# Matmuls without a reader in the last chunk's drain, and other places for the key differences

## The reference, cut to what matters

```python
x = x + attn_a(layernorm(x))   # 16 heads of 16; keys and values at offsets 0..40, 96, 128, 384 back
x = x + ffn(layernorm(x))      # 8 groups of 512 tokens: (x W1^T + b1) W2^T + b2
x = x + attn_b(layernorm(x))   # per head softmax(rope(q) rope(k)^T / 4) v over all 2048 keys
x = x + ffn(layernorm(x))
```

## Time and profile before

| | |
|---|---|
| median of 3 runs | 2109.53 us (2108.59 to 2109.8) |
| the profiled execution | 2115.02 us, span from first to last instruction 2112.9 us |
| mean granted clock | 0.965 |
| TensorE busy | 1989.9 us (94%) |
| VectorE busy | 1792.2 us (85%) |
| ScalarE busy | 1570.7 us (74%) |
| GpSimd busy | 777.9 us (37%) |
| first instruction of the second stage on TensorE | at 846.5 us |

### The profile page before, as it was taken

One profiled execution on the slowest core, in us unless ns is written; L12 is line 12 of the kernel. 1 busy time (PEld: TensorE's weight loads), 2 busy tenths in 40 slices (PEclk: granted clock), 3 DMA queues, 4 the chain that ended last, 5 costly groups with the idle time before them and its releaser, 6 DMA issues. The chain is left out here.

```text
span 2112.9 us, 48657 instructions
## 1 busy us (share of the span) xinstructions
PE 1989.9 (94%) x18498; PEld 770.3 (36%) x18498; DVE 1792.2 (85%) x3187; ACT 1570.7 (74%) x3827; POOL 777.9 (37%) x1040
## 2 busy tenths in 40 slices
PE   7889999899998786999999999999999999999978
PEld 5444555454554332222222222222222222322333
DVE  3797888788897676899999999999999999999356
ACT  0155676566664321999999999999999999999911
POOL 2599899799998310720203003003000000052100
PEclk9999999999999866899999999999999999999989
DMA  8465566566655541511102002001010010041311
GB/s 280 131 135 125 127 153 134 137 152 132 154 137 119 141 96 51 112 33 27 36 5 55 8 7 56 7 14 49 5 27 4 6 26 5 7 126 47 111 63 60
DMA packets 230728, 163.81 MB, mean 78 GB/s; under 512 B 153256, under 2 KB 201432, under 8 KB 230488
## 3 DMA queue, kind: packets, MB, share of 16 engines
q1 hardware_dynamic: 198416, 112.70, 22.2%
q0 software_dynamic: 15616, 32.02, 5.9%
q10 hardware_dynamic: 16464, 15.98, 2.3%
HBM read 98.43 MB, written 45.16 MB: 68 GB/s over the span
## 5 line engine op out<-in xcount | busy, mean ns | idle before, releaser
L1498 ACT ACTIVATE pr<-ps_s 128x512 f32<-128x512 f32 x2048 | 1042.8, 676 | 1.7 <-PE ps_s L1396 1.6
L1515 DVE TENSOR_REDUCE mx<-ps_m 128x1 f32<-128x512 f32 x1472 | 932.1, 684 | 45.3 <-PE ps_m L1373 41.5
L1414 PE MATMUL ps_o<-pr,vg 128*32 128x256 f32 x8192 | 655.0, 392 | 9.3 <-ACT f_ou L1478 8.6
L1396 PE MATMUL ps_s<-qs,ks 50*128 50x512 f16 x2048 | 612.4, 384 | 9.4 <-PEq L322 9.3
L1373 PE MATMUL ps_m<-ks,qs 48*128 48x512 f16 x1716 | 544.6, 384 | 0.0
L597 POOL TENSOR_TENSOR room<-qs 128x512 f32<-128x512 f32 x336 | 416.4, 1272 | 92.0 <-ACT qs L864 53.6
L1325 POOL DMA_DIRECT2D vg<-vb_d x24 | 19.7, 821 | 943.4 <-PE ps_o L1414 862.9
L1414 PEld LDWEIGHTS ps_o<-pr,vg 128*32 128x32 f32 x8192 | 162.5, 108 | 333.8 <-issue 210.0
L1373 PEld LDWEIGHTS ps_m<-ks,qs 48*128 48x128 f16 x1716 | 142.3, 93 | 353.3 <-issue 203.7
L943 DVE TENSOR_TENSOR room<-PSa,qs 128x512 f32<-128x512 f32 x368 | 234.4, 678 | 15.4 <-PE PSa L690 15.0
L690 PE MATMUL PSa<-room,sj 128*32 128x512 f32 x1408 | 199.1, 613 | 11.7 <-issue 4.7
(11 more groups left out here) (175 smaller groups left out, 2201.5 us busy)
## 6 DMA issues: line engine op xcount, KB each, us to landing
room<-skew SPq DMA_DIRECT2D x128, 208.0 KB, 4.0
skew<-attn SPq DMA_DIRECT2D x64, 164.0 KB, 5.0
tail_room<-in_W SPq DMA_DIRECT2D x32, 256.0 KB, 3.5
tail_room<-in_W2T SPq DMA_DIRECT2D x32, 256.0 KB, 4.1
vb_d<-vb SPq DMA_DIRECT2D x8, 1024.0 KB, 5.9
qs<-ks SPq DMA_DIRECT2D x26, 256.0 KB, 5.4
ks<-k_d POOLq DMA_DIRECT2D x48, 128.0 KB, 3.2
qs<-q_d POOLq DMA_DIRECT2D x180, 32.0 KB, 2.8
```

The source lines that it names most:

```text
L1396: pe.matmul(ps_s[:, op % SB, :], ks[rows, slot, j // 2, kt * P:(kt + 1) * P], qs[rows, q, j // 2, :], start=True, stop=True).then_inc(s_ps, 1)
L1414: mm = pe.matmul(ps_o[SLOT * j:SLOT * (j + 1), cols], vg[:, kt, j, :], pr[:, kt % PR_RING, j, cols], start=(kt == 0 and part == 0), stop=( ...
L1498: act.activation(pr[:, kt % PR_RING, j, :], ps_s[:, place_of(y, n) % SB, :], ACT.Exp, scale=exp_scale).then_inc(p_ready, 1)
L1515: dve.tensor_reduce(best, ps_m[:, n % M_BANKS, :], AX_X, ALU.max).then_inc(m_read, 1)
```

## The change

Two things. First, on ScalarE the steps `diff` go from positions 68.9 and 69 to 75.7 and 75.8, `diff_last` from 76.8 and 77.2 to 78.8 and 78.9; on VectorE `diff` goes from 71.9 and 72 to 79.5 and 80.5, `diff_rest` from 74.8 and 75 to 82 and 82.1. In whole positions ScalarE's `diff` of chunk 1 moves from 92.9 to 99.7, past `scores` 0 and 1 of chunk 4, and VectorE's from 95.9 to 103.5, past the first norm, the update and the second norm of chunk 2, and eight product slots. `diff_last` moves past `last` 0 and 1 of the next chunk.

Second, TensorE gets matmuls in chunk 7 whose result nobody reads: `identb` with itself, f16, 128 x 128, into a bank that holds nothing wanted. They stand ahead of the step's own wait: 12 before `turn` and before `pv` of units 2 to 7, 6 before `logits` of units 5 to 7 (these in `TAIL_BANK[1]`, after a wait that the values of chunk 6 are copied out of it), 20 before each `t_mean`, 30 before each `t_var` and each `t_back`, 14 before `ffn` 0 and before `qk` 0 (in `L_BANK`).

```diff
--- before.py
+++ after.py
@@ -140,7 +140,7 @@
     (32.05, "pv", 6), (33.533, "turn", 7), (37.764, "pv", 7), (39.821, "t_center", 0), (41.079, "t_var", 0),
     (45.847, "t_center", 1), (47.6, "t_var", 1), (51.942, "rotate", 0), (52.887, "rotate", 1), (54.687, "last", 0), (54.771, "last", 1), (58.502, "rotate", 2), (59.723, "values", 0),
     (60.626, "rotate", 3), (61.508, "values", 1), (67.984, "last", 2),
-    (68.079, "last", 3), (68.9, "diff", 2), (69, "diff", 3), (76.8, "diff_last", 2), (77.2, "diff_last", 3)]
+    (68.079, "last", 3), (75.7, "diff", 2), (75.8, "diff", 3), (78.8, "diff_last", 2), (78.9, "diff_last", 3)]
 DVE_STEPS = [
     (-272.989, "fold", 0), (-137.751, "fold", 1), (-49.228, "fold", 2), (-29.11, "fold", 3), (-29.109, "fold_out", 0),
     (-27.116, "fold", 4), (-24.078, "fold", 5), (-10.56, "h_add", 0), (-10.507, "fold", 6), (-9.553, "fold", 7),
@@ -158,7 +158,7 @@
     (49.232, "t_inverse", 0), (49.379, "t_normalise", 0), (50.82, "update", 0), (51.223, "t_add", 1), (51.973, "t_center", 1),
     (53.915, "t_inverse", 1), (54.806, "t_normalise", 1), (58.261, "rotate", 0), (58.524, "rotate", 1), (59.293, "rest", 0),
     (59.798, "rest", 1), (63.491, "rotate", 2), (64.094, "rotate", 3),
-    (66.977, "rest", 2), (71.781, "rest", 3), (71.9, "diff", 2), (72, "diff", 3), (74.8, "diff_rest", 2), (75, "diff_rest", 3)]
+    (66.977, "rest", 2), (71.781, "rest", 3), (79.5, "diff", 2), (80.5, "diff", 3), (82, "diff_rest", 2), (82.1, "diff_rest", 3)]
 SP_LAST = [
     (-79.26, "load_head", 0), (-32.621, "load_v64", 0), (-31.197, "skew_out", 0), (-24.258, "load_v96", 0),
     (-24.141, "skew_in", 0), (-21.558, "skew_out", 1), (-17.942, "skew_in", 1), (-13.617, "load_v96", 1),
@@ -702,8 +702,22 @@
                                        start=(k == 0), stop=(k == KC - 1))
                 return mm
 
+
+            UNIT_FILL = {"turn": (2, 12), "pv": (2, 12), "logits": (5, 6)}
+            TAIL_FILL = {"t_mean": 20, "t_var": 30, "t_back": 30, "ffn": 14, "qk": 14}
+
+            def keep_busy(bank, n):
+
+                for _ in range(n):
+                    pe.matmul(PS[:, bank, 0:P], identb[:, :], identb[:, :], start=True, stop=True)
+
             def step(j, what, i):
                 w, c, tile = j * UNITS + i, i // 4, j * TILES + i % 4
+                if j == NG - 1 and what in UNIT_FILL and i >= UNIT_FILL[what][0]:
+                    pe.wait_ge(vb_sb, 2 * j)
+                    keep_busy(TAIL_BANK[1], UNIT_FILL[what][1])
+                if j == NG - 1 and what in TAIL_FILL and (i == 0 or what[:2] == "t_"):
+                    keep_busy(L_BANK, TAIL_FILL[what])
                 if what == "fold":
                     fold(i)
                 elif what == "fold_out":
```

## The result

The changed kernel takes 2104.11 us (median of 20 runs, 2095.45 to 2108.65), the kernel before 2113.24 us (median of 20 runs on the same chip). Two of those 20 runs took 3047 and 3869 us and are left out of the ratio; the other 18 lie between 2107.0 and 2120.5. The ratio is 0.9962, with a 95% interval of 0.9951 to 0.9973: 8.0 us faster (5.7 to 10.4), where 15.6 had been forecast (the medians themselves are 9.1 apart). The sign was right and the size about half. The forecast of 2093.9 started from a median of three runs; off 2113.24 it would have been 2097.6.

What follows compares the result with a forecast made beforehand. TensorE was taken to pace chunks, with clock losses in chunk 4 and the drain. Terms -10.5 - 0.6 - 2.0 - 1.7 - 0.8 = -15.6 us off the median 2109.53 gave 2093.9 us, range 2086 to 2105.

Steps and rivals of the forecast that it cites:

- What bounds the kernel: TensorE paces a chunk at full clock; in the drain, VectorE's maximum reductions, then from `y` a chain through three engines.
- the old loss in chunk 4: Between residual adds of chunks 2 and 3: TensorE idles, then runs slow; moving the difference steps recovers 11.45 us.
- I take +1.0 us for a short wait at the turn's copy, bounds 0 and 5.0: After moving batch 0's steps, ScalarE's head-turn copy comes late; the late rotation stays covered before the second `qk`.
- Batch 1, -0.6: Only the second L1085 lies on the path, between update and half-sum; moving it saves 0.6 us.
- Turns and `pv`, -2: Idle matmuls in the last chunk's turns cut VectorE's 7.7 us idle to about 5; bounds -7 and +8.
- `y`, -1.7: Output projection: its first half runs at full clock, 1.98 us in place of 3.67.
- Norms, FFN, `qk`, -0.8: Drain after `y`: idle matmuls' cost against clock gained in both norms, FFN and `qk`; bounds -2.6 and +12.
- `t_back` +2: First norm: 30 uncovered idle matmuls cost 1.8 us, the clock perhaps down there; range +0.8 to +3.2.
- Rival 1: Chunk 4: ScalarE reaches the difference copies before VectorE made them, so most of 11.45 us stays; 2104 to 2105, chance 0.07.
- Rival 2: Drain: idle matmuls cost what they give, above all in the norms, +6 in place of -4.5; 2104, chance 0.14.
- Rival 3: Turns do not hold the clock, steps overrun: +6 in place of -2; 2101.9, chance 0.15.

Runs made afterwards that it cites:

- experiment 3: The changed kernel run once more, unaltered: ratio 0.9960 to the kernel before, residual adds of chunks 2 to 3 in 81.5 us.
- experiment 1: The kernel before with only the difference steps moved, no idle matmuls: ratio 0.9944, chunk 2 to 3 in 83.5 us.
- experiment 4: The changed kernel with ScalarE's second rotate cast moved behind the copy of `pv` 4: ratio 0.9942 to the kernel before, chunk 2 to 3 in 80.7 us.
- experiment 9: On experiment 7, batch 0's four VectorE difference instructions cut to 64 of 512 columns, ScalarE copying both halves: ratio 0.9943, chunk 2 to 3 in 78.65 us.
- experiment 11: On experiment 6, batch 0's difference steps placed in existing waits of VectorE and ScalarE: ratio 0.9919, chunk 2 to 3 in 79.2 us.
- experiment 8: On experiment 4, idle matmuls kept only before turns, `pv` and `logits`: ratio 0.9938, 62.0 us from `y` on.
- experiment 10: On experiment 6, idle matmuls before turns, `pv` and `logits` removed too, leaving means, FFN and `qk`: ratio 0.9936, 60.3 us from `y` on.
- experiment 6: On experiment 4, no idle matmuls before the variances and `t_back`s: ratio 0.9918, 2094.23 us.
- experiment 12: Experiment 6 run again unaltered: ratio 0.9919, 2093.16 us, 57.3 us from `y` on.
- experiment 5: On experiment 4, all idle matmuls removed, leaving moved steps and the later rotate cast: ratio 0.9959, chunk 2 to 3 in 80.7 us.
- experiment 7: On experiment 4, ScalarE's difference casts ahead of the fourth head's copy, VectorE's two differences back to back: ratio 0.9950, chunk 2 to 3 in 80.8 us.

## Why the prediction was right in sign and wrong in size

- **What bounds the kernel, and the old loss in chunk 4: right.** Both waits of TensorE and the 6.89 us wait of L1085 are gone with the steps moved, in every run that moves them. (The second window of rows 1 ends 0.2 us short of the residual add, so the old loss was 11.7 rather than 11.45.)
- **The step that failed: "I take +1.0 us for a short wait at the turn's copy, bounds 0 and 5.0".** It measured 83.13 - 77.45 = 5.7 us in the changed kernel, and 4.1 and 6.1 in the profiles of experiments 3 and 1, which have the same order. The prediction saw that VectorE's "5.0 us of moved work" would "push `rotate`", and that was right: it begins 10.5 us behind the second norm's L299 where it began 5.7 behind. But it followed the late rotation to one reader only, the second `qk` on TensorE, which was indeed covered. It didn't follow it through ScalarE's list: `rotate`'s casts wait for VectorE there, and the copy of `pv` 4 stands behind the second one. Experiment 4 removes that wait by one position. The casts of the differences themselves were ready, as said: L923 has no wait. What then remains, 3.3 us, is VectorE's load and its place together: taking most of that work away leaves 1.3 of it (experiment 9), laying it into waits leaves 1.8 (experiment 11). The prediction weighed each wait by itself and never set VectorE's 67 to 68 us of work per chunk, with its uneven spread, against 5 us more. What the last 1.3 us are made of stays open.
- **Batch 1, -0.6:** too small for the scatter of the drain's traces; neither shown nor refuted. In the changed kernel the differences run at 695.83 to 699.2, ahead of a wait for `qk` that shrank to 0.64 us, as described.
- **Turns and `pv`, -2: wrong, it was 0.** The price of an idle matmul was right (12 in 0.84 us at full clock), and the gaps of full-clock turns with them did come out shorter, 0.66 to 0.79 in the last ones where 1.18 to 1.34 is seen without. But the clock dropped once, at 745 to 756, as it did in every kernel with them, and there the steps cost 1.50 and 2.25 us, and earlier steps that had gaps of 0 to 0.56 now have 0.27 to 0.66. In nine profiles with the turns' idle matmuls and the moved steps VectorE waits 10.7 to 11.3 us, in three without them 10.8 to 11.4. With the steps at their old places it is 9.2 with them and 10.7 without, but the stretch is no shorter (71.9 and 71.6 us).
- **`y`, -1.7: right to the tenth,** and it is what the turns' idle matmuls buy (experiments 8 and 10).
- **Norms, FFN, `qk`, -0.8: it was +0.8.** By the prediction's terms: first norm +3.0 (variance +1.0, `t_back` +2), measured +4.0, since the half-clock case behind its bound of +3.2 came true (3.38 us for 30). FFN -2.0, measured -2.5. Second norm -0.6 (-0.95 + 1.0 - 0.65), measured +0.8: the clock had fallen there too, and its 30 in front of the variance took 3.06 us where 1.8 had been counted. `qk` -1.2, measured -1.5. What was gained at full clock was foreseen; what idle matmuls cost where they run at half clock was set too low. Experiments 6 and 12 show both norms without them: 13.1 to 13.3 and 9.3 to 9.6 us.
- **Sum.** 5.7 - 1.0 = 4.7 in chunk 4 (3.1 in the run again), 2.0 in the turns, 1.6 from `y` on: 6.7 to 8.3 us missing, of 7.6 by the ratio. These sizes are read from single traces; the ratios of whole kernels are too wide to tell the terms apart (the steps alone came to 11.8 us in experiment 1, and to 8.7 in experiment 5 with the copy moved as well, where 11.1 had been forecast).
- **Rivals.** Rival 1 (the wait moves along) is half right, by another path than its own: not at the difference casts but at the rotation's. Rival 2 (the idle matmuls cost what they give, in the norms above all) describes the norms: 60 idle matmuls per norm cost what they gave or more. That 2104 was foretold and 2104 measured is luck: it had +6 us for the drain, which got 0.9 us shorter from `y` on, and the full gain in chunk 4, of which half came. Rival 3 (turns don't hold the clock) happened in one place. The Trainium skill (TensorE: Matmul & The Clock Gate, PE-mode transpose) says that a transpose doesn't count as busy for the clock gate in the way that other matmuls do. With 12 f16 matmuls ahead of each turn the granted clock stayed at 1.00 from 720 to 744 and from 756 until `y` at 766.6, so transposes among other matmuls are no bar; no run here separates the two.

## What to carry to other kernels

When work on an in-order engine becomes late, list every reader of its results on every other engine, and for each of these what stands behind it in that engine's list; the first one found is not the one that decides. Before moving work into a stretch, set the engine's busy time there against the stretch and put it into gaps that exist.

Matmuls that only keep the clock up belong in front of an instruction for which TensorE waits anyway, and no more of them than the wait is long. Where there is no wait they are paid in full, and nearly twice when the clock is already down (30 took 1.85 us at full clock and 3.38 at half). Here 350 of them are worth nothing that can be measured, and 230 of the same 5 to 8 us by the ratios.

## What the runs showed that was not expected

- **A wait of 2.80 us that comes and goes.** In five of the fourteen profiles the stretch from chunk 4 to chunk 5 takes 80.4 to 81.8 us, in the other nine 77.2 or 77.3. Each of the five has one wait of TensorE with no other engine behind it; in the kernel of experiment 7:

```profile
576.99 1.06 PE L690 MATMUL PSa<-room,sj 128*32 128x512 f32 x8 [2.80 <-issue]
```

  Experiment 9 has a second one of 2.92 us, in an early chunk (81.9 in place of 77.4). It is found with and without the moved steps and the idle matmuls. Its cause stays open. The kernel before has it in its profile (at 589.75) and the changed kernel doesn't, so it is part of the 14.8 us between these two.
- **The same idle time doesn't always cost the clock.** The changed kernel was profiled twice, with the same 3.2 us wait of `turn` 5. In one the clock went to 0.57 for some 4 us and the stretch took 83.1; in the other it stayed at 1.00 and it took 81.5:

```profile
404.00:410.00 6.00, 3.64 (x22) 1.74 (x23) 5.93 (x10) 4.57 (x21) 5.50 (x7) 1.00 0.65 134
```

- **What an idle matmul costs.** Thirty, each with its weight load, took 1.85 us at full clock, 0.062 each, and 3.38 at half, 0.113 each. The Trainium skill (TensorE: Matmul & The Clock Gate, Back-to-back issue gap) has about 81 ns for a weight load with a 128-column matmul in a sustained stream; the trace disagrees for these f16 matmuls, and the measurement decides.
